# Matmul operands walked backwards: the split products of a one-core feed-forward and linear-attention kernel read and write their columns from last to first

## The reference

```
x = x + 0.5 * ffn(LN(x));  x = x + attn(LN(x));  x = x + 0.5 * ffn(LN(x))

ffn(x):   x_prev = x shifted by one token inside its sequence
          xr, xk = mu_r*x + (1-mu_r)*x_prev, mu_k*x + (1-mu_k)*x_prev
          return sigmoid(xr @ W_r) * (square(relu(xk @ W_k)) @ W_v)
attn(x):  q, k = relu(x Wq^T)/4, relu(x Wk^T)/4;  v = x Wv^T;  u = silu(x Wu^T)
          per head of 16 features: kv = k^T v;  out = q kv
          return (rms_norm(out per head) * u) Wo^T
```

## Time and profile before

| what | value |
|---|---|
| time, median of 3 runs | 312.8 us (312.67 to 313.02) |
| span of the profiled execution, first to last instruction | 311.3 us |
| PE busy | 303.8 us (98%), 2044 matmuls |
| DVE, ACT, POOL busy | 240.4, 235.3, 214.1 us |
| granted TensorE clock, mean | 0.997 |

### The profile page before, as it was taken

The page is one execution under the profiler, slowest core; times in us unless marked ns, Lnnn a source line. Parts: engine busy times, 40 slices in busy tenths (PEclk is TensorE's granted clock), DMA queues, the critical chain, the costliest instruction groups (busy, mean ns, idle before and its releaser), DMA issues.

```text
span 311.3 us, 5822 instructions
## 1 busy us (share of the span) xinstructions
PE 303.8 (98%) x2044; PEld 276.2 (89%) x2044; DVE 240.4 (77%) x586; ACT 235.3 (76%) x461; POOL 214.1 (69%) x236
## 2 busy tenths in 40 slices
PE   6999999999999999999999999999999999999995
PEld 5688889989988988988989998989999999999884
DVE  3989894675756846995894699586979797999695
ACT  2896959779589579679359448669797979699981
POOL 4487977779678687669169314815798979758833
PEclk9999999999999999999999999999999999999998
DMA  7970000000000000000000000000002010101134
GB/s 215 356 241 0 1 3 0 0 2 0 3 0 3 0 0 2 0 2 0 0 3 1 2 0 0 2 1 3 0 3 67 2 67 20 50 2 66 33 106 135
DMA packets 10752, 10.85 MB, mean 35 GB/s; under 512 B 482, under 2 KB 10724, under 8 KB 10724
## 3 DMA queue, kind: packets, MB, share of 16 engines
q1 hardware_dynamic: 10432, 10.23, 10.1%
q10 hardware_dynamic: 292, 0.26, 0.3%
HBM read 6.29 MB, written 4.19 MB: 34 GB/s over the span
## 4 chain that ended last, share of the span: by engine, by line
PE 89%; DVE 6%; ACT 2%; issue 1%; POOL 0%; DVEq 0%; POOLq 0%; ACTq 0%
PE psK L1270 8%; PE psK L1271 8%; PE psK L1272 8%; PE psX L1270 8%; PE psRV L1272 8%; PE psRV L1270 8%; PE psRV L1271 8%; PE psX L1271 7%; PE psX L1272 7%; PE psA L1287 4%; PE psX L1487 2%; PE psK L1474 2%; PE psA L1474 2%; PE psX L1401 2%; PE psRV L1512 1%; PE psRV L1377 1%
## 5 line engine op out<-in xcount | busy, mean ns | idle before, releaser
L939 DVE SCALAR_TENSOR_TENSOR mix<-psA,mu,mix 128x512 f32<-128x512 f32 x60 | 41.5, 744 | 11.6 <-ACT mix L626 11.6
L609 ACT ACTIVATE xn<-xs,shiftA,rstdA 128x256 f32<-128x256 f32 x53 | 27.7, 607 | 15.8 <-POOL shiftA L402 15.8
L418 POOL TENSOR_TENSOR mix_k_lo<-mix,mix_k_hi 128x512 fp32r<-128x512 f32 x26 | 33.3, 1298 | 8.7 <-ACT mix_k_hi L659 8.7
L626 ACT ACTIVATE mix<-psA,one_mu 128x511 f32<-128x511 f32 x60 | 36.9, 698 | 0.6 <-PE psA L1287 0.6
L1270 PE MATMUL psRV<-ffn_hi,mix_r_hi 128*128 128x256 f32 x120 | 34.2, 285 | 0.0
L1272 PE MATMUL psRV<-ffn_hi,mix_r_lo 128*128 128x256 f32 x120 | 33.5, 279 | 0.0
L1271 PE MATMUL psRV<-ffn_lo,mix_r_hi 128*128 128x256 f32 x120 | 33.4, 279 | 0.0
L1270 PE MATMUL psRV<-ffn_hi,act_hi 128*128 128x256 f32 x96 | 27.4, 286 | 0.0
L1272 PE MATMUL psRV<-ffn_hi,act_lo 128*128 128x256 f32 x96 | 26.8, 279 | 0.0
L1271 PE MATMUL psRV<-ffn_lo,act_hi 128*128 128x256 f32 x96 | 26.8, 279 | 0.0
L470 POOL TENSOR_TENSOR k_lo<-k_tok,k_hi 128x512 fp32r<-128x512 f32 x14 | 18.1, 1294 | 11.6 <-ACT k_hi L713 11.6
(11 more groups left out here) (204 smaller groups left out, 1084.0 us busy)
## 6 DMA issues: line engine op xcount, KB each, us to landing
xs<-x_dram SPq DMA_DIRECT2D x7, 512.0 KB, 8.6
out_dram<-xs SPq DMA_DIRECT2D x7, 512.0 KB, 3.0
out_dram<-xs SPq DMA_DIRECT2D x4, 128.0 KB, 1.8
xs<-x_dram ACTq DMA_DIRECT2D x2, 128.0 KB, 3.0
xs<-x_dram SPq DMA_DIRECT2D x2, 128.0 KB, 2.8
silu_u<-w_ffn_k_dram SPq DMA_DIRECT2D x1, 256.0 KB, 4.6
silu_u<-w_ffn_r_dram SPq DMA_DIRECT2D x1, 256.0 KB, 6.3
q_store<-w_k_dram SPq DMA_DIRECT2D x1, 256.0 KB, 6.5
```

Source lines behind the costliest of these rows:

```text
L418: nc.gpsimd.tensor_tensor(mix_k_lo[:, h, :], mix[:, 0, h, :], mix_k_hi[:, h, :].bitcast(F32), ALU.subtract).then_inc(s_lo_k, 1)
L609: nc.scalar.activation(xn[:, t, :], tile_row(xs, b, t), ACT.Identity, bias=shiftA[:, t:t + 1], scale=rstdA[:, t:t + 1]).then_inc(s_xn, 1)
L626: nc.scalar.activation(mix[:, rk, h, 1:BLOCK], psA[:, h, 0:BLOCK - 1], ACT.Copy, scale=one_mu[:, rk, h:h + 1]).then_inc(s_prev, 1)
L939: nc.vector.scalar_tensor_tensor(out=m, in0=psA[:, h, :], scalar=mu[:, rk, h:h + 1], in1=m, op0=ALU.mult, op1=ALU.add).then_inc(s_mix, 1)
```

## The change

Inside PE's program a small function turns an access pattern round: over its one free dimension, or over both where it has two. product() applies it to the destination in PSUM and to the two moving operands. Column 511 (or 255) is then read first and written first, column 0 last. Both sides are turned, so each result stands in the place where it stood. The stationary operands, all other matmuls, the order of instructions, the waits and the semaphores are as before.

```diff
@@ -1266,7 +1266,11 @@
 
         @block.tensor
         def _(pe):
+            def from_the_end(ap):
+                return ap[:, ::-1] if len(ap.shape) == 2 else ap[:, ::-1, ::-1]
+
             def product(dst, a_hi, a_lo, b_hi, b_lo, start, stop):
+                dst, b_hi, b_lo = (from_the_end(ap) for ap in (dst, b_hi, b_lo))
                 nc.tensor.matmul(dst, a_hi, b_hi, start=start, stop=False)
                 nc.tensor.matmul(dst, a_hi, b_lo, start=False, stop=False)
                 return nc.tensor.matmul(dst, a_lo, b_hi, start=False, stop=stop)
```

## The result

The changed kernel takes 315.27 us (314.96 to 316.22, 5 runs) against 313.02 us of the kernel before (5 runs): ratio 1.0068, 95% interval 1.0046 to 1.0090. It is slower by 2.2 us, a small difference but clear of the noise. The forecast was no change. The profiled execution took 314.96 us, with a span of 313.2 us against 311.3.

The account below looks back on a forecast made before the run. The prediction took PE, streaming the products, to bound the kernel. It priced walking downwards and a cost at each matmul's start at zero, so the forecast stayed at the time of before, 312.8 us; full range 312 to 520 us.

Parts of the forecast that it names:

- What bounds the kernel: Whole kernel: PE bounds it, 89% of the chain; between about 10 and 280 us product time is kernel time.
- The count of columns and the distances: Products: 1548 matmuls, 516,096 columns; starts 117.5 ns apart at 256 columns, 233.8 at 512, so 0.454 ns a column.
- I take zero for both: Products: walking downwards (-19 to +202 us, farther +662) and a cost at each matmul's start (0 to +128 us) both priced zero.
- Rival 2: Each product matmul: first fetch or write starts later, 5 ns each, 7.7 us in all, giving 320.5 us; chance 0.12.
- Neither sign of the prediction: Product starts: equal surplus at 256 and 512 columns would show a per-matmul cost, twice as much at 512 a stream cost.
- Rival 1: Product streams: a step of -1 forms no pairs, so columns take 0.85 ns, +202 us, giving 513 us; chance 0.34.
- rival 5: Products: they fall to the price of plain float32 ones, giving 975 us; chance 0.02.
- Rival 3: Product streams: the 10% over the clock comes from ascending order and vanishes downwards, -19 us, giving 293.5 us; chance 0.06.

Follow-up runs that it names:

- the bench: Kernel computing nothing of the reference, with streams of 24 product matmuls on PE alone; 256 columns start every 120.0 ns upwards, 118.4 with reading turned.
- three layouts: Turned products with operands as before, behind 128 unused bytes, or with four gaps: ratios to the kernel before 1.0068, 1.0036, 1.0034; the latter two upwards 0.9969, 0.9958.

## Why the prediction was wrong

1. **What bounds the kernel**: right in the main. A cost in the products came out in the time, but 3.1 us of it as 2.0 of PE's run; "every nanosecond" of a product was a third too much.
2. **The count of columns and the distances**: the counts are right. The two distances were each taken at one place, 16 and 8 matmuls, and stood for all kinds. Here the error began. The earlier trace rows already had it: 279 ns for most products of 256 columns, 282 for gram and 278 for ffn_v into psX; 395 and 394 for 512. A record lasts 161 to 163 ns longer than its distance, and the distances of these very rows are 117, 119, 115, 234 and 231 ns. For k_and_u even that hid something, as the group is one line of three: L1270 and L1272 lie mostly at 229 and 226 ns. Nor do two distances show a price per column: a slope and a remainder fit any two points. With gram's 119.5 and k_and_u's 229.1 ns they would be 0.428 and 9.9 in place of 0.454 and 1.3, and the bench has 128 columns at 111.8 ns, where 0.454 and 1.3 would give 59.4.
3. **"I take zero for both"**: this is the step that failed, for the read. Its reason was that the stream costs 0.454 ns a column "whichever tensor it reads the earlier trace rows". It does not. Reading downwards costs +2.7 ns a matmul in ffn_r, +4.3 in k_and_u, -1.0 in gram and nothing in ffn_k, 2.0 ns in the mean over the 1548. That is inside the bounds that the text gave, and the term was set to zero. For writing downwards zero was right.
4. **Rival 2, a small cost per matmul**, had the sign, and 315.27 us lies within its bounds of 313.5 and 441. It took 5 ns a matmul and 7.7 us; measured are 2.0 ns a matmul before waits took some up, 1.3 after, and 2.2 us. That its bounds hold the time is luck, since its mechanism, a later first fetch, doesn't fit: at 128 columns nothing is added, at 384 and 512 4.4 and 5.5 ns, at 256 in the same bench something is won. Neither sign of the prediction appeared, the same surplus at 256 and 512 columns or twice as much.
5. **Rival 1, half rate**, was far off: 120 ns, not 218 (and rival 5, far slower, still more). Turned streams stood between 5% under (126.3 to 120.0) and 6% over (113.3 to 120.0) the same stream upwards, in no case near double. The Trainium skill, page "SBUF — State Buffer", section "Door 1: The DMA port swizzle", says that consecutive accesses to a line of 16 bytes run at full bandwidth once there are two to a line. The prediction took this to hold in either direction; the runs bear that out to within these 6%, and no farther.
6. **Rival 3, faster**, was argued against with "it doesn't vary between tensors and banks, as a collision would". It does vary, from 113.3 to 120.0 ns in the kernel before, and the surplus over one column per clock can be won back in part, by places and upwards. Downwards, gram won 1.0 ns.
7. The range of 312 to 520 us held the time, but this says little; nearly all of its width was for a mechanism that isn't there.

Shown: the cost is all in reading the moving operand downwards; it adds up by kinds of product; its size, and at 256 columns its sign, depend on where the moving and the stationary operand start, modulo 256 bytes; the short cadences (113.3 and 226.7 ns) were reached upwards only, at the places tried. Not settled: what in the chip makes these cadences. Other engines needn't be at work for them, the weights' start and number count, and a collision of the two reads was argued but not shown. Why a unit of the kernel holds 113.3 or 117.8 ns at the same addresses is open too.

## What to carry to other kernels

Where PE sets the time, read the distance between starts for every kind of matmul, not for one stretch: kinds that differ by 2 to 4 ns at equal shapes have something to win or lose. Read the moving operand of a dense float32r stream in ascending order unless its own distances say otherwise (turning cost 0.7 to 0.8% in three layouts, though gram alone gained); write PSUM in whichever order suits. Unused bytes between operands are a cheap thing to try (here 0.3 to 0.4%), but how much of it arrives is decided by the next chain, and the same few bytes shift every operand allocated behind them.

## What the runs showed of the hardware

- A float32r matmul of 256 columns started every 113.3 to 127 ns at the granted clock of 1.00 (the 2.4 GHz level), with nothing changed but direction, the start of its operands by bytes and the number of stationary columns; 512 columns every 226.7 to 240 ns; 128 columns every 111.8 ns, hardly less than 256.
- With 128 stationary columns the cadence followed the difference of moving and stationary start modulo 256 bytes, in steps of 64 bytes (moving + 192 like stationary + 64, both 113.3 ns; moving + 256 like none, 120.0). A start off a multiple of 16 bytes gave the slowest streams (126.3 ns at 8 bytes) but also one of the faster (116.8 at 12).
- Writing a PSUM bank from its last column to its first cost nothing (ratio 0.9994, 0.9982 to 1.0006).
- At difference 0 the number of stationary columns (128, 64, 32) gave 120.0, 113.3 and 117.9 ns upwards at 256 columns and 226.7, 230.0 and 231.2 at 512.
- Distances settle into repeating patterns, mostly after a handful of matmuls; behind one wait a stream that had run at 113.3 ns went on at 117.8 (ffn_v of unit 14 in the kernel before).
